# Three split-precision products for the routed values, and the router scores in column groups

## The reference

```
x   = rbf_attention(x)                 # 16 heads of 8 features, exp(-gamma * distance), masked
x   = x + local(ln(x)) ; x = routed(x) # "f1": local windowed attention, then routed attention
x   = x + ssm(rms(x))                  # state-space scan
x   = x + local(ln(x)) ; x = routed(x) # "f2": the same block again

def route(x, token, num):              # x is the normalised sequence
    s = x @ token                      # the router score of each token
    50 times: a = logk - logsumexp(s + b);  b = -relu(s + a)
    return top_k(exp(s + a + b), num)  # 64 queries, 128 contexts per sequence

def heavy_attn(xq, ctx, ...):
    q = rms(xq) @ Wq.T;  k, v = split(rms(ctx) @ Wkv.T)
    o = softmax(q @ [null, k].T * scale) @ [null, v]
    return o @ Wout.T
```

## Time and profile before

| what | us |
|---|---|
| median of three runs | 1855.6 (1853.57 to 1856.98) |
| the profiled execution, its own time | 1859.21 |
| span of the profiled execution | 1857.4 |
| PE busy | 1684.3 (91%) |
| DVE busy | 1448.5 (78%) |
| ACT busy | 1436.0 (77%) |
| POOL busy | 753.7 (41%) |

### The profile page before, as it was taken

The page is one execution under the profiler, slowest core; times in us unless marked ns, Lnnn a source line. Parts: engine busy times, 40 slices in busy tenths (PEclk is TensorE's granted clock), DMA queues, the critical chain, the costliest instruction groups (busy, mean ns, idle before and its releaser), DMA issues. The chain is left out here.

```text
span 1857.4 us, 67964 instructions
## 1 busy us (share of the span) xinstructions
PE 1684.3 (91%) x27513; PEld 1292.5 (70%) x27513; DVE 1448.5 (78%) x3468; ACT 1436.0 (77%) x4092; POOL 753.7 (41%) x842
## 2 busy tenths in 40 slices
PE   3888899886999999999997996989999999999797
PEld 1444444443688888888886774658888888888686
DVE  8999999998577778777887766747777777789574
ACT  4989999996588888888774666668888888877464
POOL 2010000000145444545445866425454545455685
PEclk7999999998999999999999998999999999999999
DMA  6655555551001010101012000000000010101211
GB/s 196 147 142 149 151 132 136 143 141 24 13 14 26 14 26 14 26 14 26 14 24 49 2 2 1 1 12 20 20 20 20 16 23 17 23 14 25 48 46 47
DMA packets 80040, 91.94 MB, mean 49 GB/s; under 512 B 11697, under 2 KB 67985, under 8 KB 79729
## 3 DMA queue, kind: packets, MB, share of 16 engines
q1 hardware_dynamic: 78432, 87.15, 19.2%
q10 hardware_dynamic: 1296, 0.44, 0.1%
HBM read 39.68 MB, written 31.10 MB: 38 GB/s over the span
## 5 line engine op out<-in xcount | busy, mean ns | idle before, releaser
L1497 POOL TENSOR_TENSOR f1l_pn<-f1l_p,f1l_rs 128x512 f32<-128x512 f32 (+1 forms) x256 | 207.9, 834 | 259.6 <-DVE f1l_rs L1185 258.6
L1497 POOL TENSOR_TENSOR f2l_pn<-f2l_p,f2l_rs 128x512 f32<-128x512 f32 (+1 forms) x256 | 207.9, 834 | 250.7 <-DVE f2l_rs L1185 250.7
L1065 ACT ACTIVATE f2l_p<-f2l_sm,f2l_nb 128x192 f32<-128x192 f32 x512 | 214.4, 443 | 44.5 <-DVE f2l_nb L1178 44.5
L1065 ACT ACTIVATE f1l_p<-f1l_sm,f1l_nb 128x192 f32<-128x192 f32 x512 | 214.5, 443 | 42.4 <-DVE f1l_nb L1178 42.4
L412 PE MATMUL r_acc<-r_pr,r_vp 128*32 128x128 f32 (+2 forms) x3584 | 193.3, 332 | 6.6 <-DVE r_pr L625 5.5
L522 ACT ACTIVATE r_pr<-r_far 128x1536 f32<-128x1536 f32 x128 | 194.7, 1521 | 2.9 <-PE r_far L396 2.6
L617 DVE SCALAR_TENSOR_TENSOR r_pr<-r_pr,k_lo,r_cap 128x512 f32<-128x512 f32 x256 | 179.8, 743 | 9.0 <-ACT r_pr L522 8.8
L625 DVE TENSOR_SCALAR r_pr<-r_pr,k_hi,k_lo 128x768 f32<-128x768 f32 x256 | 163.1, 678 | 0.0
L522 ACT ACTIVATE r_pr<-r_near 128x1024 f32<-128x1024 f32 x128 | 138.9, 1085 | 1.4 <-PE r_near L383 1.3
L1502 POOL MEMSET k_rtz<- 128x608 f32 x1 | 0.6, 605 | 334.3 <-POOLq L683 334.3
L1178 DVE TENSOR_REDUCE f2l_nb<-f2l_sm 128x4 f32<-128x768 f32 x128 | 116.0, 947 | 7.5 <-PE f2l_sm L885 7.5
(11 more groups left out here) (503 smaller groups left out, 5173.4 us busy)
## 6 DMA issues: line engine op xcount, KB each, us to landing
rbf_rows<-r_part SPq DMA_DIRECT2D x112, 128.0 KB, 2.2
r_qs<-rbf_rows SPq DMA_DIRECT2D x60, 192.0 KB
r_ks<-rbf_rows SPq DMA_DIRECT2D x60, 192.0 KB
f1l_vs<-f1l_vv SPq DMA_DIRECT2D x64, 128.0 KB, 2.4
f2l_vs<-f2l_vv SPq DMA_DIRECT2D x64, 128.0 KB, 2.4
rbf_rows<-r_part SPq DMA_DIRECT2D x16, 384.0 KB, 3.0
rbf_rows<-r_part SPq DMA_DIRECT2D x16, 256.0 KB, 3.1
out<-k_x SPq DMA_DIRECT2D x8, 512.0 KB, 3.2
```

What stands on the lines that cost most here:

```text
L1065: ins = nc.scalar.activation(p[:, u % 2, k, :], sm[:, u % 2, k // 2, k % 2 * PW:(k % 2 + 1) * PW], ACT.Exp, bias=nb[:, u % 2, k:k + 1], ac ...
L1497: ins = nc.gpsimd.tensor_tensor(pn[:, u % 2, at:at + HU * w].rearrange("p (k c) -> p k c", k=HU), p[:, u % 2, :, cols], r.broadcast_to([P, ...
```

## The change

1. The contents product becomes three float32r products that add up in one bank: low tokens by high weights, high tokens by low weights, high by high. ACT makes the high tokens `gh` from `gx` right behind `gx`, DVE the low tokens `gl = gx - gh` (`low_tokens`), and PE waits for `gl`. The weights are split in the RBF stage as a fourth part of the loop that splits `wqkv`; their plain load in `K["later"]` is gone.
2. The stationary matrix of the router scores has 32 columns. Sequence b goes to column group b % 4, and the scores are issued four at a time, once four turned sequences lie in `yt`, which has four buffers instead of two. The rows of the router lie therefore on all 128 partitions at 32 * (b % 4) + b // 4 (and 4 more for the second score), and every router and choosing operation takes 128 partitions with as many elements in each as before. The places leave in four transfers, and the four transposes take 128 rows.
3. In the opening of f1, ACT scales the rows of sequences 1 and 2 by an activation with scale and bias, ahead of `leave_x(0)`. DVE makes the bias in one more small operation, ahead of `rows(0)`, and scales sequence 3 where it scaled 1.

The core of the diff:

```diff
 def contents(m):
     wait(pe, v_x, m - 1)
+    pe.wait_ge(v_gl, m + 1)
     for h in range(2):
-        nc.tensor.matmul(W_[:, XB + h, :], gx[:, h, NQ:], K["wv_h"][:], start=True,
+        nc.tensor.matmul(W_[:, XB + h, :], gl[:, h, :], K["wv_hh"][:], start=True, stop=False)
+        nc.tensor.matmul(W_[:, XB + h, :], gh[:, h, :], K["wv_hl"][:], start=False, stop=False)
+        nc.tensor.matmul(W_[:, XB + h, :], gh[:, h, :], K["wv_hh"][:], start=False,
                          stop=True).then_inc(p_v, 1)
...
     nc.scalar.activation(gx[:], ...).then_inc(a_x, 1)
+    act.wait_ge(a_x, m + 1)
+    nc.scalar.activation(gh[:], gx[:, :, NQ:], ACT.Copy).then_inc(a_gh, 1)
...
+def low_tokens(m):
+    dve.wait_ge(a_gh, m + 1)
+    wait(dve, p_v, 2 * m)
+    nc.vector.tensor_tensor(gl[:], gx[:, :, NQ:], gh[:], ALU.subtract).then_inc(v_gl, 1)
...
 if 1 <= n <= M:
     reciprocals(n - 1, 1)
+if n < M:
+    low_tokens(n)
 if n >= 2:
     residual(n - 2)
...
 def score_rows(b):
     pe.wait_ge(s_ye, b + 1)
-    nc.tensor.matmul(xa[:, 1, :], K["rtz"][:, 2 * B * b:2 * B * b + P], yt[:, b % 2, :],
-                     start=b == 0, stop=b == B - 1).then_inc(s_ss, 1)
+    q, i = b % RG, b // RG
+    nc.tensor.matmul(xa[32 * q:32 * q + 32, 1, :], K["rtz"][:, 32 * i:32 * i + 32], yt[:, q, :],
+                     start=i == 0, stop=i == RI - 1, skip_group_check=True).then_inc(s_ss, 1)
...
 for b in range(B):
-    score_rows(b)
+    if b % RG == RG - 1:
+        for back in range(RG):
+            score_rows(b - RG + 1 + back)
...
+act.wait_ge(s_d, 7)
+for b in OURS:                       # OURS = (1, 2)
+    for t in range(NT * b, NT * (b + 1)):
+        ins = nc.scalar.activation(K["y"][:, t, :], K["x"][:, t, :], ACT.Identity,
+                                   scale=K["rstd"][:, t:t + 1], bias=vy[:, t:t + 1])
+    ins.then_inc(s_ya, 1)
...
-if 0 <= p - 2 < N:                   # state space: scores after outputs(p)
-    score(2 * (p - 2))
-    score(2 * (p - 2) + 1)
+if 0 <= p - 2 < N and p % 2:
+    for q in range(RG):
+        score(2 * (p - 3) + q)
...
-for q in range(3):                   # RBF stage, POOL
+for q in range(4):
     w = slice(THIRD * q, THIRD * (q + 1))
+    high, low = (K["wqkv_h"][:, w], K["wqkv_l"][:, w]) if q < 3 else (K["wv_hh"][:], K["wv_hl"][:])
     pool.wait_ge(s_wl, 16 * (q + 1))
```

More of the change, by code:

```diff
@@ L65, in host_constants @@
     rows = np.zeros((P, 4), f)
-    k = np.array([NQ] * B + [NKV] * B, np.float64)
-    rows[:2 * B, 0] = -np.log(np.minimum(k * FETCH, S).astype(f))
-    rows[:2 * B, 1] = k
-    rows[:2 * B, 2] = k + 1
-    rows[B:2 * B, 3] = 1
+    kv = np.arange(P) % 32 // 4 == 1
+    k = np.where(kv, NKV, NQ).astype(np.float64)
+    rows[:, 0] = -np.log(np.minimum(k * FETCH, S).astype(f))
+    rows[:, 1] = k
+    rows[:, 2] = k + 1
+    rows[:, 3] = kv
     c["router_rows"] = rows
@@ L332, in _ @@
                 batch(b, b % 2)
-                if 0 <= b - SPLIT_AT < 3:
+                if 0 <= b - SPLIT_AT < 4:
                     q = b - SPLIT_AT
                     wait(sp, s_wh, 2 * q)
-                    sp.dma_start(whole[:], A["wqkv"][:, THIRD * q:THIRD * (q + 1)]).then_inc(s_wl, 16)
+                    src = A["wqkv"][:, THIRD * q:THIRD * (q + 1)] if q < 3 else A["wv_h"]
+                    sp.dma_start(whole[:], src).then_inc(s_wl, 16)
                 for dst, src in K["later"][LATER * max(b - B + RUN, 0):LATER * max(b + 1 - B + RUN, 0)]:
@@ L775, in stage_light @@
         SEARCH = B - 4
-        R2 = 2 * B
         LASTK = 2 * (NKV // 8) + 6
-        picks = sb("picks", [R2, S])
-        some = sb("some", [R2, S])
-        one = sb("one", [R2, 1])
-        top = sb("top", [R2, 8])
+        picks = sb("picks", [P, S])
+        some = sb("some", [P, S])
+        one = sb("one", [P, 1])
+        top = sb("top", [P, 8])
         s_tk = sem("tk")
@@ L958, in turn_rows @@
             def turn_rows(b):
-                pe.wait_ge(s_y, b + 1)
+                if b in OURS:
+                    pe.wait_ge(s_ya, OURS.index(b) + 1)
+                else:
+                    pe.wait_ge(s_y, b + 1 - sum(o < b for o in OURS))
                 wait(pe, s_ye, b - 1)
@@ L1097, in leave_rows @@
                 act.wait_ge(s_yy, b + 1)
-                wait(act, s_ss, b - 1)
-                nc.scalar.activation(yt[:, b % 2, :], tp[:] if b % 2 == 0 else xa[:, 0, :], ACT.Copy).then_inc(s_ye, 1)
+                wait(act, s_ss, b - RG + 1)
+                nc.scalar.activation(yt[:, b % RG, :], tp[:] if b % 2 == 0 else xa[:, 0, :], ACT.Copy).then_inc(s_ye, 1)
             if C:
@@ L1378, in _ @@
                 link(nc.vector.reciprocal(K["r2"][:], two[:, 0, :]))
-                rows(1)
+                rows(3)
                 split_first()
-                for b in range(2, 9):
+                for b in range(4, 9):
                     rows(b)
@@ L2157, in leave_result @@
                 act.wait_ge(s_yt, 2 * q + e + 1)
-                wait(act, s_sc, 2 * q + e - 1)
-                a(yt[:, e], ty[:], ACT.Copy).then_inc(s_ye, 1)
+                wait(act, s_sc, 2 * q + e - RG + 1)
+                a(yt[:, (2 * q + e) % RG], ty[:], ACT.Copy).then_inc(s_ye, 1)
             def result(q):
@@ L2261, in score @@
                 pe.wait_ge(s_ye, b + 1)
-                nc.tensor.matmul(srow[:], K["rtz"][:, 2 * B * b:2 * B * b + P], yt[:, b % 2, :],
-                                 start=b == 0, stop=b == B - 1).then_inc(s_sc, 1)
+                q, i = b % RG, b // RG
+                nc.tensor.matmul(srow[32 * q:32 * q + 32, :], K["rtz"][:, 32 * i:32 * i + 32], yt[:, q, :],
+                                 start=i == 0, stop=i == RI - 1, skip_group_check=True).then_inc(s_sc, 1)
             for p in range(-AFTER, N + AFTER):
@@ L2295, in program @@
             load(n, A["c_" + n], [P, A["c_" + n].shape[1]])
-        for n in ("wout_l", "wq_h", "wk_h", "wv_h", "wout_h"):
+        for n in ("wout_l", "wq_h", "wk_h", "wout_h"):
             load(n, A[n], [P, H * DH])
```

69 lines of the change are left out of this document (42 added, 27 removed).

## The result

The changed kernel is slower. Its median is 1868.5 us (1862.9 to 1874.7, 10 runs), that of the kernel before in the same runs 1860.0 us (1853.6 to 1866.3, 10 runs); ratio 1.0047, 95% interval 1.0031 to 1.0063. Forecast were 1845 us and a chance of 0.03 for slower. The profiled execution has a span of 1867.4 us in place of 1857.4, and a mean clock of 0.967 in place of 0.976.

A forecast was written before the change was run, and what follows sets the result against it. Each place had its own bound: DVE in RBF, PE in routed attention and f1's opening, PE and ACT by turns in state-space. -6.8 - 4.5 + 1.75 - 2.2 + 1.0 = -10.75 us, from median 1855.6 to 1845; 8-in-10 range 1839 to 1851.

The forecast's parts named there:

- The opening of f1: First local attention: scores in column groups save 7.45 us, leave_x(0) comes 0.65 later; net -6.8 us, bounds -9.2 and -4.
- The state-space stage: One score group of 1.05 us every second step replaces two scores of 1.82 us each step; net -4.5 us, bounds -2 and -8.
- then the chain over statistics, `result` and turn_result sets the end, and no more comes: State-space stage, after the step p = 5: this chain sets the end, so the gain stops growing; net -4.5 us.
- The walk itself: State-space stage, step by step from p = 2: 1.8 us earlier, then 3.6 at p = 4 and 4.4 at p = 5.
- rival D: Opening and state-space stage: PE's pauses drop its clock from 2.4 to 1.2 GHz, state-space +29 us, about 1892; chance 0.03.
- The contents product in f1: Routed attention of f1: PE gains 0.35 us a round, but five rounds wait for nulls, +0.56 each; sum +1.75 us.
- f2: Routed attention of f2: DVE's 2.23 us to spare hides the delay; eight rounds gain 0.35, 0.1 returned in six; -2.2 us.
- I take 0.64, and 0.57 until the residual can start: Routed attention, DVE's low-token subtraction beside POOL: priced at 0.64 us, delaying the residual by 0.57.
- rival B: Routed attention: low tokens delay DVE 1.7 us, f1 +5.3 us, f2's gain eaten by slower POOL; 1850.6 us, chance 0.19.
- The residual and all behind it on DVE come 1.0 us later: Routed attention: ACT's copy (0.43 us) and DVE's subtraction (0.57) shift later DVE work by 1.0 us, bounds 0.6 and 1.3.
- the sum of the loop: f1's routed attention, loop from gather through nulls to output: 12.66 - 0.44 + 1.0 = 13.22 us, against PE's 12.31.
- The fourth split: RBF stage: two DVE operations beside a split last 2.22 us in place of 1.26; +1.0 us, bounds 0 and +1.8.

The follow-up runs named there:

- the kernel with the maxima first: Changed kernel with low tokens computed from PSUM and DVE's order nulls, statistics, maxima, places: 1849.8 us, ratio 0.9962 to the kernel before.
- the old scores: The kernel with the maxima first, its state-space scores again one 128-column float32 matmul per sequence, two a step: 1849.0 us, ratio 0.9955 to the kernel before.
- the low tokens from PSUM: Changed kernel with low tokens computed from the gathered tokens in PSUM, one SBUF input, DVE's order unchanged: 1861.9 us, ratio 1.0026 to the kernel before.
- the kernel with both changes: Changed kernel with null_query waiting on POOL for DVE's places, and low tokens computed from PSUM: 1852.2 us, ratio 0.9972 to the kernel before.
- contents alone: The kernel before with only the split contents product, gh, low tokens and fourth split, scores keeping 128 stationary columns: 1873.3 us, ratio 1.0066.
- scores alone: Changed kernel with one float32 contents product, without gh, gl and fourth split; score groups and ACT's row scaling stay: 1853.2 us, ratio 0.9955 to the kernel before.

## Why the prediction was wrong

**The opening of f1: right.** -6.5 us against -6.8. A group takes 1.07 us (forecast 1.05). That the sum is so near is partly luck. The stretch that I had walked through went from 25.96 us to 19.78 (474.62 to 494.40), 6.2 less and not 7.45: ACT waited 1.6 and 2.5 us at two groups, more than I had allowed. Two other terms made it good. `leave_x(0)` comes 0.26 us later after the stage's start, not 0.65; everything ahead of it came 0.4 us sooner, since DVE's first operation beside POOL's clearing of `rtz` took 0.21 us in place of 0.61, the clearing of the shorter `rtz` 0.21 in place of 0.60, and the prediction had put that at nothing. And the first turned sequence came 10.33 us behind `leave_x(0)` in place of 10.89, which I did not follow up. Of the 1.6 us lost in the rest of that stage I know that the clock fell once between 600 and 620, where in the kernel before it had fallen between 500 and 510; over fourteen traces of all the kernels this part takes 505.2 to 508.0 us, so it may be no more than scatter.

**The state-space stage: wrong, -4.5 forecast, +0.7 measured.** The step that failed is "then the chain over statistics, `result` and turn_result sets the end, and no more comes": the sum kept the 4.5 us to the end and took all of PE's work at full clock. The walk itself was good: "1.8", "3.6" and "4.4" were 1.8, 3.6 and 4.3 us in the kernel with the maxima first, against the old scores, and then the waits of 2.56 and 3.31 us and the slow clock behind them took all of it. In the changed kernel two slow stretches came before that, at the outputs of pairs 2 and 4 (3.50 and 3.66 us for 2.06), so that its outputs of pair 6 start at 76.5 us where the kernel before has 76.9; the first of the two has nothing to do with the groups. The mechanism was in the prediction, as rival D, with a chance of 0.03 and a price of 29 us; it came in small. The argument against it (PE busy 1.53 of 4 us and the clock at 1.00) was taken from the very waits of 2.48 and 2.03 us behind which the clock falls in other traces of the same step, so one trace could not carry it.

**The contents product in f1: wrong, and it decided.** The forecast had the product and the copy about right: contents 1.57 us for 1.47, a gain of 0.25 to 0.31 a round for 0.35 (the rounds of f2 fell from 12.66 to 12.35). The steps that failed are two.

First, "I take 0.64, and 0.57 until the residual can start". The subtraction took 1.4 us in three of the eight rounds, and in five with the clock kept up by idle products. That is rival B's mechanism, with the Trainium skill's rule behind it ("SBUF — State Buffer", "Who interferes with whom": the loser waits for the whole instruction); this case's runs agree with it: 0.41 us alone, 1.45 beside POOL's 1.27, and 0.47 with one input in PSUM. The row that I set against it (0.64) was an operation with other inputs. But this step alone cost little: short subtractions in the same order brought 0.2%, hardly clear of the noise.

Second, and this is the cause: "The residual and all behind it on DVE come 1.0 us later", taken as a shift of fixed durations. `places` had been 0.87 us ahead of `null_query`. With the low tokens from PSUM the delay was 0.43 + 0.47 = 0.90 us, less than my own 1.0, and it came behind all the same, by 0.23; so the forecast's own number led there. Then the loop gets POOL's chain in it: a round of 14.73 us at full clock, whatever the subtraction takes. The prediction named the slack of nulls and of the normalisation, and did not look at what stands on POOL beside the last DVE operation before nulls. By its own sum, rounds were to be 13.2 us; where neither operation meets POOL they are 12.8 (the kernel with both changes, for which the same sum gives 13.05). So the sum of the loop was near and its premise was not. It is not exact: `places` took 0.45 us in that kernel and 1.07 in the loop that the sum began from, so that with all its terms right the sum would have been 12.22 + 0.90 - 0.62 = 12.5.

Beside these two, a term that the sum did not have: what follows from a long wait. With waits of 0.3 to 0.7 us a round the clock stayed at 1.00; in the changed kernel it fell behind each of the three waits of 2.2 to 2.3 us, and that made 3.9 us in this stage. Rival D had been placed in the opening and in the state-space stage alone. In the opening it did not happen: 1.00 from 470 to 500.

**f2: right**, -2.6 for -2.2, with the same -2.6 for contents alone and 118.6 us, as before, for scores alone. DVE had the slack of the earlier trace rows, as said: the subtraction took 1.37 us there in five rounds, and they still were 12.35 us.

**The fourth split: open.** +1.0 us in this pair of traces, but over the twelve traces with that split this stage ended between 453.3 and 458.5 us, and without it at 456.4 in the kernel before and at 451.8 with scores alone. The scatter is larger than the term, and that the pair gave the forecast's +1.0 is luck.

**The range** reached to 1851 and left out a case in which two of the rivals, B and D, come together in the one stage whose slack was 0.44 us.

## What to carry to other kernels

Before an operation is pushed back on VectorE, look at what GpSimd does at the old and at the new time: a large elementwise instruction there is a gate, and the question is whether the operation still gets through ahead of it, not how much later it comes. Price the wait that results, then ask again what a wait of that length does to TensorE's clock; if the order can't be changed, a few idle matmuls placed inside the wait kept the clock here (1.66 us of them in the routed attention, twice 1.9 in the state-space stage), where 0.9 us behind the outputs did not. And a clock that stayed up behind a pause in one trace is no proof that it will: look at the same place in several. And put what the next stage waits for ahead of what only has to be ready some time, here nulls and maxima ahead of `places`.

## What the runs showed of the hardware

A tensor_scalar with one tensor as its input, in SBUF, stood behind GpSimd's tensor_tensor as well: 0.45 us alone, up to 2.40 us beside a 2.35 us instruction. I had expected this of two-input operations only. The held operation ended 0.28 us behind GpSimd's, for tensor_scalar and for tensor_tensor alike. Taking one such wait away, 1.45 to 0.47 us, lengthened the next ones by as much: the onehots (L1911) 1.09 to 1.52 and `places` 1.70 to 2.40.

In the changed kernel TensorE's clock fell to 1.2 GHz behind waits of 2.2 to 2.3 us in rounds in which it was otherwise busy all the time, and the work behind ran slow for some 7 us; with 1.66 us of idle products in the same waits it stayed at 2.4 GHz. In the contents-only kernel the clock fell behind only two of four waits of that length, and with the low tokens from PSUM behind two of three, so the length of one wait does not settle it.
